# A transformer tower on one core: q, k and v from one-hot products with folded tables, 1/sigma turned by TensorE

## The reference, cut to what matters

```python
nesting, segments = _syntax_info(token_ids)            # from cumulative sums over the tokens
combined = concat([pos_table[pos], nest_table[nesting], seg_table[segments]], -1)
h = combined @ W                                       # (32, 512, 128)
qkv = (layernorm(h) @ qkv_w.T + qkv_b).reshape(b, s, 8, 3, 16)
attn = softmax(einsum('bshc,bthc->bhst', q, k) / 4)    # 8 heads of 16
h = h + einsum('bhst,bthc->bshc', attn, v).reshape(b, s, 128) @ out_w.T + out_b
x = layernorm(h)                                       # then 4 gated experts:
hidden = relu(einsum('ni,ehi->neh', x, fc1_w))         # fc1, then two low-rank factors and fc2
h = h + sum_e weights[n, e] * expert_out[n, e]         # weights from a softmax minus a sigmoid
```

## Time and profile before

| | us |
|---|---|
| median of 3 runs (1199.28 to 1201.93) | 1199.8 |
| the profiled execution | 1200.39 |
| its span from first to last instruction | 1198.6 |
| PE busy | 1112.8 |
| DVE busy | 910.2 |
| ACT busy | 823.0 |
| POOL busy | 592.8 |
| start of the first exponential (ACT L507) | 91.51 |
| mean of an exponential of 128x512 (ACT L507) | 0.598 |
| mean of a product of two float32 tiles of 128x512 (POOL L460) | 1.271 |

### The profile page before, as it was taken

The page is one execution under the profiler, slowest core; times in us unless marked ns, Lnnn a source line. Parts: engine busy times, 40 slices in busy tenths (PEclk is TensorE's granted clock), DMA queues, the critical chain, the costliest instruction groups (busy, mean ns, idle before and its releaser), DMA issues.

```text
span 1198.6 us, 20409 instructions
## 1 busy us (share of the span) xinstructions
PE 1112.8 (93%) x6392; PEld 455.6 (38%) x6392; DVE 910.2 (76%) x2370; ACT 823.0 (69%) x1602; POOL 592.8 (49%) x588
## 2 busy tenths in 40 slices
PE   2579999999999999999999999999999999999975
PEld 1223334444344434434344444443443444433322
DVE  6288888877888788777888887778888877788322
ACT  0217777777777777777777777777777777777841
POOL 2644555456544555565445655654455555622231
PEclk9669999999999999999999999999999999999997
DMA  3534534545454345454444455444444454441111
GB/s 84 130 81 97 123 88 113 120 110 123 103 120 105 102 106 119 116 120 105 117 107 102 102 120 125 111 107 114 112 102 100 118 127 109 109 102 44 54 56 36
DMA packets 88377, 123.98 MB, mean 103 GB/s; under 512 B 17469, under 2 KB 69054, under 8 KB 82054
## 3 DMA queue, kind: packets, MB, share of 16 engines
q1 hardware_dynamic: 86720, 121.08, 43.0%
q10 hardware_dynamic: 1550, 1.59, 0.5%
HBM read 80.81 MB, written 34.95 MB: 97 GB/s over the span
## 4 chain that ended last, share of the span: by engine, by line
PE 59%; DVE 20%; issue 4%; DMA 1%; POOL 1%; ACT 0%; SPq 0%; POOLq 0%; DVEq 0%
PE pv L635 14%; PE mix L645 12%; PE sc L624 11%; DVE negmax L882 11%; PE mix L697 7%; PE mix L662 4%; PE mix L713 3%; PE mix L702 2%; PE mix L680 2%; PE mix L657 2%; DVE out_sb L961 2%; DVE rden L901 1%; PE mix L673 1%; DVE onehot L861 1%; DVE mres L892 1%
## 5 line engine op out<-in xcount | busy, mean ns | idle before, releaser
L882 DVE TENSOR_REDUCE negmax<-mix 128x1 f32<-128x512 f32 x1024 | 669.9, 680 | 173.3 <-PE mix L645 166.2
L507 ACT ACTIVATE probs<-sc 128x512 f32<-128x512 f32 x1024 | 576.8, 598 | 183.8 <-PE sc L624 179.4
L624 PE MATMUL sc<-qstk,kstk 120*128 120x512 bf16 x1024 | 366.8, 381 | 0.8 <-ACT probs L507 0.6
L645 PE MATMUL mix<-kstk,qstk 96*128 96x512 bf16 x1024 | 357.2, 392 | 10.0 <-DVE negmax L882 4.8
L635 PE MATMUL pv<-probs,vals 128*32 128x512 f32 x2048 | 274.0, 601 | 0.0
L645 PEld LDWEIGHTS mix<-kstk,qstk 96*128 96x128 bf16 x1024 | 99.7, 98 | 347.2 <-DVE negmax L882 198.1
L460 POOL TENSOR_TENSOR ctxh<-ctx_sb,rdenb 128x512 f32<-128x512 f32 x64 | 81.3, 1271 | 258.7 <-DMA rdenb<-rden_dram 258.2
L624 PEld LDWEIGHTS sc<-qstk,kstk 120*128 120x128 bf16 x1024 | 99.5, 98 | 106.1 <-issue 36.6
L697 PE MATMUL mix<-xn2T,fc1T_sb 128*128 128x512 f32 x256 | 131.9, 599 | 0.0
L416 POOL TENSOR_TENSOR hb_sb<-h_sb,obias 128x512 f32<-128x512 f32 x32 | 40.7, 1273 | 121.6 <-DVE h L907 121.6
L565 ACT ACTIVATE hid<-mix 128x512 f32<-128x512 f32 x128 | 76.8, 600 | 24.2 <-PE mix L697 24.2
(11 more groups left out here) (116 smaller groups left out, 1067.8 us busy)
## 6 DMA issues: line engine op xcount, KB each, us to landing
stack_dram<-pieces SPq DMA_DIRECT2D x192, 128.0 KB
rdenb<-rden_dram SPq DMA_DIRECT2D x64, 256.0 KB
qstk<-stack_dram SPq DMA_DIRECT2D x32, 384.0 KB, 6.6
kstk<-stack_dram SPq DMA_DIRECT2D x32, 384.0 KB, 8.7
qstk<-stack_dram SPq DMA_DIRECT2D x32, 256.0 KB, 6.9
kstk<-stack_dram SPq DMA_DIRECT2D x32, 256.0 KB, 9.3
wrow<-w_dram SPq DMA_DIRECT2D x32, 256.0 KB
out<-out_sb SPq DMA_DIRECT2D x32, 256.0 KB, 2.7
```

The costliest lines, as they stand in the source:

```text
L507: act.activation(probs[:, c % 8, i % 2], sc[:, i % RING], ACT.Exp).then_inc(s_exp, 1)
L624: pe.matmul(sc[:, i % RING, :], kstk[0:KROWS, u, h, j * P:(j + 1) * P], qstk[0:KROWS, u, h, :], start=True, stop=True).then_inc(s_score, 1)
L645: pe.matmul(max_bank(m), qstk[0:STK, u, h, j * P:(j + 1) * P], kstk[0:STK, u, h, :], start=True, stop=True).then_inc(s_mxmm, 1)
L882: dve.tensor_reduce(negmax[:, m // NT, m % NT:m % NT + 1], max_bank(m), AX.X, ALU.max, negate=True).then_inc(s_max, 1)
```

## The change

- The layer norm is linear in h but for 1/sigma, and h is a table row plus a position row. So the centred product with the weights of q, k and v is folded in the set-up into three more one-hot tables and into position terms (posQK, posV). In the steps q, k and v come from the one-hot operand directly, as bfloat16 products of 96 rows; the normalised rows, their turning and its copy are gone.
- DVE adds the position terms of q and k out of PSUM (`add_qk`), POOL multiplies them with 1/sigma (`scale`), and ACT then adds the bias from SBUF. ACT copies v out; POOL adds its position term and multiplies twice (`value`).
- To multiply q and k, 1/sigma must lie along the free axis on all partitions. PE turns the four columns beside the maxima (`turn_rstd`), ACT copies them out (`copy_rT`), SP stores them (`rstd_out`) and loads them broadcast (`rstd_in`, 256 KB).
- The embedding moves from slot 11 to slot 1; q, k, v are made one step earlier, in slots 9, 13, 15; fc1_3 moves to slot 2 of the next step, slot 4 is empty, and the turning of the maxima uses slot 11's bank and not slot 12's. DVE's position sum and statistics move from slots 11 to 13 to slots 2 to 5, the one-hot comparison from slot 9 to the end of the step before.
- SP's list stores k's first piece before the denominators, and has the store and load of 1/sigma between the gate weights and the stacks. POOL's list begins with `scale`.
- In the set-up come nine float32 fold groups, their copies by ACT, and a second table cut by DVE; POOL waits for the last of them before its first step.

```diff
 PRODUCTS = [
-    ("project", -2), ("xnT", 3), ("q", 3), ("low", -3), ("k", 3), ("xn2T", -2), ("out", -3), ("gates", -2),
-    ("turn_gates", -2), ("v", 3), ("fc1_0", -2), ("embed", 4), ("mT", 1), ("fc1_1", -2), ("fc1_2", -2), ("fc1_3", -2),
+    ("project", -2), ("embed", 4), ("fc1_3", -3), ("low", -3), ("none", None), ("xn2T", -2), ("out", -3), ("gates", -2),
+    ("turn_gates", -2), ("q", 4), ("fc1_0", -2), ("mT", 1), ("fc1_1", -2), ("k", 4), ("fc1_2", -2), ("v", 4),
...
-BESIDE = {3: 3, 7: 7, 11: 12}
+BESIDE = (3, 7, 11)
 ACT_WORK = [
-    (1, 1, "xnT", 3, 0), (2, 1, "qk", 3, 0), (4, 0, "ctx", -1, 1), (4, 2, "qk", 3, 1), (5, 2, "xn2T", -2, 0),
-    (8, 0, "gates", -2, 0), (9, 0, "gate_exp", -2, 0), (9, 1, "v", 3, 0), (10, 1, "relu", -2, 0),
-    (12, 0, "mT", 1, 0), (12, 0, "ctx", 0, 0), (12, 1, "wT", -2, 0), (13, 1, "relu", -2, 1), (14, 1, "relu", -2, 2),
-    (15, 1, "relu", -2, 3),
+    (1, 2, "qk", 3, 0), (2, 2, "relu", -3, 3), (3, 1, "qk", 3, 1), (4, 0, "ctx", -1, 1), (5, 2, "xn2T", -2, 0),
+    (8, 0, "gates", -2, 0), (9, 0, "gate_exp", -2, 0), (10, 1, "relu", -2, 0),
+    (12, 0, "mT", 1, 0), (12, 0, "ctx", 0, 0), (12, 1, "wT", -2, 0), (12, 1, "rT", 4, 0), (13, 0, "relu", -2, 1),
+    (14, 1, "relu", -2, 2), (15, 2, "v", 4, 0),
 ]
 DVE_WORK = [
     (0, 1, "add_attention", -2, 0), (1, 0, "stats2", -2, 0), (1, 1, "stats2", -2, 1), (2, 0, "moments2", -2, 0),
-    (4, 0, "weigh", -3, 0), (6, 1, "finish", -3, 0), (7, 1, "invert_den", -1, 0), (8, 1, "gate", -2, 0),
-    (9, 1, "gate", -2, 1), (9, 2, "hot", 4, 0), (10, 0, "gate", -2, 2), (10, 0, "gate", -2, 3),
-    (11, 1, "add_pos", 4, 0), (12, 0, "stats1", 4, 0), (12, 1, "stats1", 4, 1), (13, 0, "moments1", 4, 0),
+    (2, 1, "add_pos", 4, 0), (3, 0, "stats1", 4, 0), (3, 1, "stats1", 4, 1), (4, 0, "weigh", -3, 0),
+    (5, 0, "moments1", 4, 0), (6, 1, "finish", -3, 0), (7, 1, "invert_den", -1, 0),
+    (8, 1, "gate", -2, 0), (9, 1, "gate", -2, 1), (10, 0, "gate", -2, 2), (10, 0, "gate", -2, 3),
+    (10, 1, "add_qk", 4, 0), (14, 0, "add_qk", 4, 1), (15, 2, "hot", 5, 0),
 ]
 POOL_WORK = [
-    ("add_bias", 3, 0), ("rstd2", -2, 0), ("norm2", -2, 0), ("second", 3, 0), ("residual", 3, 0), ("third", 3, 0),
-    ("second", 3, 1), ("residual", 3, 1), ("third", 3, 1), ("normalise", -1, 0), ("rstd1", 4, 0), ("norm", 4, 0),
+    ("scale", 3, 0), ("add_bias", 3, 0), ("scale", 3, 1), ("rstd2", -2, 0), ("norm2", -2, 0),
+    ("second", 3, 0), ("residual", 3, 0), ("third", 3, 0), ("rstd1", 4, 0),
+    ("second", 3, 1), ("residual", 3, 1), ("third", 3, 1), ("normalise", -1, 0), ("v", 3, 0),
 ]
 SP_WORK = [
-    ("ids", 4, 0), ("piece", 3, (0, 0)), ("den_out", -1, 1), ("piece", 3, (0, 1)), ("piece", 3, (0, 2)),
-    ("den_in", -1, 0), ("piece", 3, (1, 0)), ("piece", 3, (1, 1)), ("out", -3, 0), ("piece", 3, (1, 2)),
-    ("rden_out", -1, 0), ("rden_in", -1, 0), ("den_out", 0, 0), ("max_in", 1, 0), ("weights_out", -2, 0),
-    ("weights_in", -2, 0), ("stack", 3, 0), ("stack", 3, 1),
+    ("ids", 5, 0), ("piece", 3, (0, 0)), ("piece", 3, (1, 0)), ("den_out", -1, 1), ("piece", 3, (0, 1)), ("den_in", -1, 0),
+    ("piece", 3, (0, 2)), ("out", -3, 0), ("piece", 3, (1, 1)), ("rden_out", -1, 0), ("piece", 3, (1, 2)),
+    ("rden_in", -1, 0), ("den_out", 0, 0), ("max_in", 1, 0), ("weights_out", -2, 0), ("rstd_out", 4, 0),
+    ("weights_in", -2, 0), ("rstd_in", 4, 0), ("stack", 3, 0), ("stack", 3, 1),
...
+            def store_rstd(b):
+                upto(sp, s_rT, b)
+                upto(sp, s_rstdin, b - 1, 16)
+                sp.dma_start(rstd_dram, rT).then_inc(s_rstdout, 16)
+            def load_rstd(b):
+                upto(sp, s_scaled, b - 1, 2)
+                upto(sp, s_rstdout, b, 16)
+                sp.dma_start(rstdb[:], rstd_dram.rearrange("j p -> (j p)").partition_broadcast(P)).then_inc(s_rstdin, 16)
...
+            def rstd_first(b):
+                upto(pool, s_v, b - 2, 2)
+                upto(pool, s_rTmm, b - 2)
+                rstd(b, mv1, ve1, rstd1[:, b % 2], s_mv1, s_ve1, s_rstd1)
...
+            def scale(b, side):
+                upto(pool, s_rstdin, b, 16)
+                upto(pool, s_raw, b, 2, side + 1)
+                pool.tensor_tensor(qk32[:, side, :], qk32[:, side, :], rstdb[:], ALU.mult).then_inc(s_scaled, 1)
+            def value(b, u):
+                upto(pool, s_v32, b)
+                pool.tensor_tensor(v32[:], v32[:], posV[:].rearrange("p j (h c) -> p j h c", h=NH),
+                                   ALU.add).then_inc(s_vpos, 1)
+                upto(pool, s_vpos, b)
                 upto(pool, s_rstd1, b)
-                pool.tensor_tensor(hc[:], h_sb[:], mv1[:, :, 0:1].broadcast_to([P, NT, P]),
-                                   ALU.subtract).then_inc(s_hc, 1)
-                upto(pool, s_hc, b)
-                upto(pool, s_xnTmm, b - 1)
-                pool.tensor_tensor(xn[:], hc[:], rstd1[:].unsqueeze(2).broadcast_to([P, NT, P]),
-                                   ALU.mult).then_inc(s_xn, 1)
+                upto(pool, s_pv, b - U, 8)
+                for g, col in ((0, 0), (1, HC)):
+                    pool.tensor_tensor(vals[:, u, :, 4 * g:4 * g + 4, col:col + HC], v32[:, :, 4 * g:4 * g + 4],
+                                       rstd1[:, b % 2].unsqueeze(2).unsqueeze(3).broadcast_to([P, NT, 4, HC]),
+                                       ALU.mult).then_inc(s_v, 1)
...
+            pool.wait_ge(s_pos, 3)
...
+            act.wait_ge(s_foldmm, 1)
...
+            for side in range(2):
+                act.wait_ge(s_fold2mm, 2 + side)
+                act.copy(posQK[:, side, :], sc[:, 1 + side]).then_inc(s_pos, 1)
+            act.wait_ge(s_fold2mm, 4)
+            act.copy(posV[:], pv[:].rearrange("p (j n) -> p j n", j=NT)).then_inc(s_pos, 1)
+            act.copy(kstk[STK:KROWS, 0, :, :],
+                     const_sb[STK:KROWS, 4:4 + NH].unsqueeze(2).broadcast_to([3 * NH, NH, S])).then_inc(s_const, 1)
...
-                upto(act, (s_qmm, s_kmm)[side], b)
-                upto(act, s_pc1, b - 1, 2, side + 1)
-                upto(act, s_res0, b - 1, 2, side + 1)
-                act.activation(qk32[:, side, :], aux("qk"[side], 1), ACT.Identity,
-                               bias=(qb_sb[:], qkb_sb[:, 1:2])[side], scale=(QSCALE, 1.0)[side]).then_inc(s_qk32, 1)
+                upto(act, s_scaled, b, 2, side + 1)
+                act.activation(qk32[:, side, :], qk32[:, side, :], ACT.Identity,
+                               bias=(qb_sb[:], qkb_sb[:, 1:2])[side]).then_inc(s_qk32, 1)
                 upto(act, s_qk32, b, 2, side + 1)
                 upto(act, s_pcout[side], b - 1, 48)
                 act.copy(pieces[:, side, 0, :], qk32[:, side, :]).then_inc(s_pc0, 1)
...
+            def copy_rT(b):
+                upto(act, s_rTmm, b)
+                upto(act, s_rstdout, b - 1, 16)
+                act.copy(rT, aux("mT", 1)[2 * Q:2 * Q + NT, 0:P]).then_inc(s_rT, 1)
...
+            def fold_positions():
+                for side in range(2):
+                    pe.matmul(sc[:, 1 + side], qkvC[:, side], posWT, start=True, stop=True).then_inc(s_fold2mm, 1)
+                for j in range(NT):
+                    mm = pe.matmul(pv[:, j * P:(j + 1) * P], posWT[:, j * P:(j + 1) * P], qkvC[:, 2], start=True, stop=True)
+                mm.then_inc(s_fold2mm, 1)
...
             def qk(b, side):
-                upto(pe, s_xnT, b)
-                pe.matmul(aux("qk"[side], 1), qkvT_sb[:, side, :], xnT[:], start=True, stop=True).then_inc((s_qmm, s_kmm)[side], 1)
+                upto(pe, s_hot, b)
+                if b == 0:
+                    pe.wait_ge(s_table, 2)
+                pe.matmul(aux("qk"[side], 1), table[:, 1 + side], onehot[:], start=True, stop=True).then_inc((s_qmm, s_kmm)[side], 1)
             def v(b):
-                upto(pe, s_xnT, b)
+                upto(pe, s_hot, b)
                 for j in range(NT):
-                    mm = pe.matmul(aux("v")[:, j, :], xnT[:, j * P:(j + 1) * P], qkvT_sb[:, 2, :], start=True, stop=True)
+                    mm = pe.matmul(aux("v")[:, j, :], onehot[:, j * P:(j + 1) * P], table[:, 3], start=True, stop=True)
                 mm.then_inc(s_vmm, 1)
...
+            def turn_rstd(b):
+                upto(pe, s_rstd1, b)
+                pe.matmul(aux("mT", 1)[2 * Q:2 * Q + NT, 0:P], rstd1[:, b % 2], id32[:],
+                          start=True, stop=True).then_inc(s_rTmm, 1)
...
-                "q": (lambda b: qk(b, 0), (s_qk32, 2, 1)),
-                "k": (lambda b: qk(b, 1), (s_qk32, 2, 2)),
-                "v": (v, (s_v, 2, 2)),
+                "q": (lambda b: qk(b, 0), (s_raw, 2, 1)),
+                "k": (lambda b: qk(b, 1), (s_raw, 2, 2)),
+                "v": (v, (s_v32, 1, 1)),
...
+                    if name == "none":
+                        return -1, (s_h, 1, 1)
+                    if name == "mT" and runs(t + 4):
+                        return t + 4, (s_rT, 1, 1)
...
+                    if t == -4 and c == 2:
```

(16 more changed lines are left out.)

154 lines of the change are left out of this document (96 added, 58 removed).

## The result

The changed kernel takes 1268.8 us (median of 4 runs, 1266.7 to 1270.6) against 1200.5 for the kernel before on the same chip: a ratio of 1.057, 95% interval 1.055 to 1.059. The forecast was 1219, with a range up to 1245. It named the right sign, and missed most of the loss.

A forecast was written before the change was run, and what follows sets the result against it. PE was taken as the bound by sum, with DVE meeting it in slots 8 to 11. Forecast: 1200.4 + 12 (denominators' loop) + 10 (front) - 3 (ends) = 1219 us, range 1197 to 1245.

The forecast's parts named there:

- PE's net saving: PE, per step: 3.38 us of work gone, 0.96 added, net -2.42; removed waits in slots 11 and 5 another -0.5.
- q's sum: Slot 10: PE's second maximum must wait for DVE's q sum, behind DVE's unbroken run; new wait 1.7 us a step.
- Position sum: Slot 2: PE's second maximum must wait for DVE's position sum; new wait 0.85 us a step.
- ACT's copy of 1/sigma: Slot 12: PE's second maximum waits for ACT's rT, queued behind wT; 0.3 us a step.
- Ring of the step: Steady step from PE's savings and new waits on DVE and ACT: 34.05 to 34.2 us, taken as 34.1.
- Rival (c): Waits of 1.7 and 0.85 don't come, DVE being there in time: step 31.5, time 1142 us; chance 0.10.
- Rival (e): Waits of 1.7 us in every step might drop PE's clock to 1.2 GHz for two slots: 1300 us; chance 0.03.
- the cover of 0 to 2.4 us: Slack between POOL's scale of q, after 1/sigma's load lands, and ACT's need; if gone, ACT and PE wait.
- SP's loop over the denominators: Denominators, queued behind k's first piece, land at 605.5, DVE wants 605.1: 0.4 us per step, +12 us.
- rival (a): Denominators are in time: step stays at 34.1, the cost is the front, 1207 us; chance 0.22.
- Front: Set-up up to the first exponential: k's stack at about 65 instead of 51.1; +10 us, between +4 and +16.
- The ends: First full-load steps and last ones: two shorter by 3 to 4 us together, one longer by some 1; -3 us.

The follow-up runs named there:

- e3: Changed kernel without 1/sigma's turning, copy, store and load, POOL scaling by ones (q and k lack 1/sigma): 1201.6 us, ratio 1.000.
- e4: Changed kernel with 1/sigma's store and load kept, but POOL scales by ones without waiting for the load: 1226.7 us, ratio 1.020.
- e5: Changed kernel with SP issuing both stacks' loads before the small stores and loads instead of after them: 1421.2 us, ratio 1.183.
- e17: Changed kernel with POOL's third piece of k beginning only when DVE has cut the maxima: 1248.1 us, ratio 1.039.
- e11: Changed kernel, POOL's bias sum first, DVE's two sums early, head rows early, ACT's q addition a slot later, 1/sigma's transfers ahead of gate weights': 1214.3 us.
- e18: e12 with POOL's third piece of k beginning only when DVE has cut the maxima: 1154.2 us, ratio 0.960.
- e2: Changed kernel with DVE's position sum at the head of slot 2 and q's sum at the head of slot 10: 1264.9 us, ratio 1.053.
- e12: e2 without 1/sigma's turning, store, load and wait (q and k lack 1/sigma): 1200.6 us, ratio 1.000.
- e14: e12 with DVE's two casts of the maxima's pieces written as two-operand operations: 1208.0 us, ratio 1.006.

## Why the prediction was wrong

**Right in the main.** PE's net saving and the removed waits would be handed to DVE's order. The saving was forecast at 2.4; a step without PE's waits took 33.5 us before and takes 31.4 in the changed kernel, so it is 2.1. q's sum: forecast 1.7, measured 1.56. Position sum: forecast 0.85, measured 0.68 in e3, where nothing else delays it. ACT's copy of 1/sigma: 0.3, measured 0.17. Ring of the step: forecast 34.1, measured 34.0 in e3, which is in part luck: e3 lacks the turning (0.08) and ACT's copy (0.3), so its own forecast would be 33.7, and e4, which has both, takes 34.4. The ring was too low by 0.3. Rival (c), the faster one, needed DVE to reach q's sum earlier; no trace has that without a changed order.

**Rival (e), the clock, came in small.** The mean waits of 1.2 to 1.6 us left it at 1.00 in most steps. Behind longer ones, 2.46 and 1.97 us, it fell twice in the 25 steady steps, 1.6 us each, and twice in the first three; 1300 was far off. With waits of 3.4 us and more in a step, in e5, it cost as much as the added waits.

**The step that failed: the load of 1/sigma, priced at nothing.** Its time to landing was bounded at 2.1 to 4.5 and measured at 6.3, so the cover of 0 to 2.4 us was gone. The larger fault is who stands behind it: I asked when ACT wants the scaled q, and not what is queued behind the scaling on POOL. There the bias sum stood, with DVE's position sum behind it and PE behind that. The part of the step, by medians: 34.9 in e17 against 34.0 in e3, 0.9 us, made of 0.74 for the position sum (1.42 against 0.68) and 0.17 for ACT's copy. Over the 25 steps it is 28.5 us (879.8 against 851.3), since e17 also has the four slow steps and e3 none.

**A cost not thought of: POOL's lateness puts its operations beside DVE's cut.** 35.7 to 34.9, 0.8 us a step by medians, 16.4 us over the 25 steps (e17). I had written that POOL's added work is hidden by its idle time. As waiting time it was; as a neighbour of DVE it wasn't. In the kernel before no operation was held like this in the 12 steps from 600 to 1000 us; in e3, with all of POOL's added work but not its wait, the first cast's mean rises only from 188 to 228 ns.

**SP's loop over the denominators, +12 us, did not bind.** Store to load takes 2.14, and the inversion doesn't wait. In that point rival (a) was right. Even at a step of 33.7, in e11, DVE waits for them only 0.4. The sum came as near as it did because this wrong term stood for part of a missing one.

**Front, +10 forecast, 17.9 measured, and 9.4 more in the first three steps.** The parts came as forecast until the load: `posV` is copied at 27.0, the head rows take 3.6 (the forecast's 3.5 doesn't follow from 0.598 for 512 elements, which gives 4.8 for 4096), ACT's copy of 1/sigma starts at 33.7. The scaling was then put at 38 and starts at 40.5, since store and load take 3.3 and 3.2; the k stack at 65 and PE goes on at 68.5:

```profile
68.52 1.44 PE L716 MATMUL mix<-kstk,qstk 96*128 96x512 bf16 x3 [15.08 <-DMA kstk<-stack_dram]
```

The 4 us that the maxima behind it were to save didn't come: 40.9 us from there to the first exponential, 40.4 before. PE's granted clock there is 0.50, its lower level of 1.2 GHz, where it was 0.58 before. Of the first three steps' 9.4 us, 8.1 go with the trip (89.8 in e3); their granted clock is 0.90, 1.00 and 0.95 (0.98, 1.00 and 1.00 in e3). The ends gave 0.2 instead of 3.

Left open: of e4's 25 us (trip kept, not waited for), how much is traffic, how much SP's issue and how much the lower clock in its first steps, since nothing separated them; and a version with the trip, e11's orders and e18's wait in one, the likeliest to beat the kernel before, wasn't tried.

## What to carry to other kernels

When a change puts a wait into an engine's list, price everything queued behind it on that engine and the readers of that; the intended reader is often the last to suffer. An engine with idle time is not free: look where its operations come to lie in time beside DVE's casts and two-operand operations, since POOL's lateness there cost 16 us beside the 28 of the wait itself, and one added wait on POOL gave the 16 back. A longer wait can cost twice, as in e5: once as idle time and once more in a lower clock behind it, so read the granted clock of every run whose step grew. Small transfers that others wait for go ahead of the large burst, and a saving on the busiest engine in a ring is had only when every other order in the ring is opened with it: e2, e12 and e14 each left one of them closed and gained next to nothing over the same kernel without the edit.

## What the runs showed of the hardware that was not expected

- A DVE operation of 0.19 us that starts just after a POOL operation of 1.16 us begins takes 0.9 to 1.2 us and ends with it, casts and two-operand operations in SBUF alike.
- From the issue of an 8 KB store to the issue of the load that waits for it took 2.4 us ahead of the stack loads, and 6.9 us behind 1.5 MB of them (e5, a kernel 12% slower than the changed one, half of that by the clock).
- A load of 256 KB, the same 2 KB row to all 128 partitions, landed after 3.2 us in the first step and 6.3 in the steady ones, issued just ahead of the stacks; with one more load between it and the stacks (e11) after 4.1, and with the stacks ahead of it (e5) after 5.3.
- PE's granted clock fell to its lower level right behind single waits of 1.7 to 2.5 us, though not behind every one of that size, with PE about 90% busy in the mean: in 2 of the changed kernel's 25 steady steps and 4 of e17's. Such a step took 1.6 to 2 us more.
